# Row sums of the attention by padded ones on TensorE

## The reference

```python
q = _split_heads(query @ Wq.T + bq)      # 16 heads of 8 columns
scores = jnp.einsum('bhqd,bhkd->bhqk', q, k) / np.sqrt(D_K)
p_attn = jax.nn.softmax(scores, axis=-1)
attn = jnp.einsum('bhqk,bhkd->bhqd', p_attn, v)
x = attn.transpose(0, 2, 1, 3).reshape(B, S, D_MODEL)
return x @ Wo.T + bo
```

## Time and profile before

| what | value |
|---|---|
| runs | 1197.23, 1201.19, 1213.32 us; median 1201.19 us |
| profiled execution, its own time | 1206.03 us |
| its span, first to last instruction | 1204.3 us |
| mean granted TensorE clock | 0.878 |
| PE busy | 958.4 us (80%) |
| DVE busy | 793.0 us (66%) |
| ACT busy | 627.6 us (52%) |
| POOL busy | 579.4 us (48%) |

### The profile page before, as it was taken

The page is one execution under the profiler, slowest core; times in us unless marked ns, Lnnn a source line. Parts: engine busy times, 40 slices in busy tenths (PEclk is TensorE's granted clock), DMA queues, the critical chain, the costliest instruction groups (busy, mean ns, idle before and its releaser), DMA issues.

```text
span 1204.3 us, 18225 instructions
## 1 busy us (share of the span) xinstructions
PE 958.4 (80%) x5148; PEld 693.5 (58%) x5148; DVE 793.0 (66%) x2660; ACT 627.6 (52%) x1875; POOL 579.4 (48%) x637
## 2 busy tenths in 40 slices
PE   6440699993787888888879889888888888888883
PEld 6220588882564665566656556566656656665552
DVE  3526467653585786887789678778867867764342
ACT  2631466652344765655556556565655656643440
POOL 2477533333655347537446644744654444532223
PEclk9975799997897999989989988998998988996775
DMA  9799587661601002021011102101110200200000
GB/s 273 240 365 346 195 282 254 253 227 53 80 1 29 8 5 39 5 38 28 14 17 26 36 8 36 36 7 28 23 29 7 35 10 8 39 10 7 7 5 5
DMA packets 126519, 93.70 MB, mean 78 GB/s; under 512 B 77546, under 2 KB 105684, under 8 KB 121684
## 3 DMA queue, kind: packets, MB, share of 16 engines
q1 hardware_dynamic: 121268, 82.05, 24.9%
q0 software_dynamic: 4096, 8.40, 2.6%
q10 hardware_dynamic: 1056, 2.10, 0.6%
HBM read 59.46 MB, written 33.06 MB: 77 GB/s over the span
## 4 chain that ended last, share of the span: by engine, by line
PE 48%; DVE 19%; POOL 15%; issue 8%; ACT 7%; DMA 2%; SPq 0%; DVEq 0%; POOLq 0%; ACTq 0%
PE U L1140 5%; POOL xs_dram L526 5%; PE U L1144 5%; PE U L1141 5%; PE M L1349 4%; PE M L1343 4%; PE M L1376 4%; DVE xin L977 3%; ACT pr L779 3%; PE Y L1140 2%; PE M L1388 2%; PE Y L1144 2%; PE Y L1141 2%; PE U L1150 2%; PE OA L1361 2%
## 5 line engine op out<-in xcount | busy, mean ns | idle before, releaser
L587 POOL TENSOR_TENSOR h_lo<-h,h_hi 128x512 fp32r<-128x512 f32 x128 | 165.7, 1294 | 230.9 <-ACT h_hi L750 230.8
L779 ACT ACTIVATE pr<-M,nmax 128x128 f32<-128x128 f32 x512 | 180.4, 369 | 77.8 <-DVE nmax L1078 77.5
L1078 DVE CUSTOM_DVE_ANT_0 M<-M,mneg 128x128 f32<-128x128 f32 x512 | 132.4, 320 | 48.8 <-PE M L1343 47.8
L784 ACT ACTIVATE pT<-M 128x512 f32<-128x512 f32 x128 | 76.5, 598 | 137.1 <-PE M L1349 137.0
L1140 PE MATMUL U<-xn_hi,w_hi 128*128 128x512 f32 x256 | 130.9, 511 | 10.6 <-DVE h L1018 5.8
L1018 DVE SCALAR_TENSOR_TENSOR h<-h,U 128x512 f32<-128x512 f32 x128 | 87.4, 683 | 56.4 <-ACT h L744 56.3
L1349 PE MATMUL M<-ident,pr 128*128 128x128 f32 x512 | 96.3, 318 | 34.6 <-ACT hqT L801 18.0
L1141 PE MATMUL U<-xn_hi,w_lo 128*128 128x512 f32 x256 | 112.3, 439 | 0.0
L1144 PE MATMUL U<-xn_lo,w_hi 128*128 128x512 f32 x256 | 112.2, 438 | 0.0
L750 ACT ACTIVATE h_hi<-h 128x512 fp32r<-128x512 f32 x128 | 81.8, 639 | 48.4 <-DVE h L1022 46.8
L779 ACT ACTIVATION_READ_ACCUMULATOR pr<-M,nmax 128x1 f32 x512 | 106.8, 209 | 0.0
(11 more groups left out here) (308 smaller groups left out, 2308.8 us busy)
## 6 DMA issues: line engine op xcount, KB each, us to landing
wt<-w_dram SPq DMA_DIRECT2D x23, 1024.0 KB, 4.8
w_dram<-wt SPq DMA_DIRECT2D x8, 1024.0 KB, 7.7
xs_dram<-xr SPq DMA_DIRECT2D x1, 5888.0 KB, 19.7
ys_dram<-acc SPq DMA_DIRECT2D x12, 256.0 KB, 2.3
key_stack<-k_dram SPq DMA_DIRECT2D x48, 64.0 KB
wt<-k_dram SPq DMA_DIRECT2D x48, 64.0 KB
ys_dram<-part SPq DMA_DIRECT2D x11, 256.0 KB, 2.1
pr<-in_L_xattn_W SPq DMA_DIRECT2D x8, 256.0 KB, 6.2
```

The source lines that it names most:

```text
L587: nc.gpsimd.tensor_tensor(h_lo[i % 4][:, :], h32[i % 3][:, :], h_hi[i % 4][:, :].bitcast(fp32), ALU.subtract).then_inc(lo_done, 1)
L779: done = nc.scalar.activation(pr[i % 2][:, c], bank[:, c], ACT.Exp, bias=nmax[i % 4][:, r:r + 1], scale=-1.0, accum_out=rsum[b % 2][:, HB ...
L784: nc.scalar.activation(pT[i % 2][:, :], bank[:, :], ACT.Copy).then_inc(emptied, 1)
L1078: ins = nc.vector.tensor_tensor_reduce(bank[:, c], bank[:, c], mneg[i // HB % 2][:, :], 1.0, BIG, ALU.add, ALU.min, nmax[i % 4][:, r:r + 1])
```

## The change

A tile `ones_pad` of 24 + 32 columns is made once at the start by GpSimd: zeros, with ones in 8 columns. In each `pv` step four more matmuls follow the four products: their stationary operand is a block of 32 columns of `ones_pad` that has its 8 ones where head j of the group stands, their moving operand is the same piece of `pT`, and they write the second 128 columns of `OA`. After the four quads each of the 128 output rows has its row's sum beside it. `o` then takes the reciprocal of these 128 x 128 sums from PSUM into `rT` and multiplies. The accumulation in `exp`, the steps `rs` and `rT`, their tiles and their waits are gone.

```diff
@@ pools, POOL start
-        rsum, rinv, rwide = [sb(f"rsum{i}", [P, H]) for i in range(2)], sb("rinv", [P, H]), sb("rwide", [P, H, DK])
+        ones_pad = sb("ones_pad", [P, VPAD + CG])
...
+            nc.gpsimd.memset(ones_pad[:, :], 0.0).then_inc(ones_made, 1)
+            pool.wait_ge(ones_made, 1)
+            nc.gpsimd.memset(ones_pad[:, VPAD:VPAD + DK], 1.0).then_inc(ones_made, 1)
@@ ScalarE
-                    b, j = i // HB, i % HB
-                    if j == 0 and b >= 2:
-                        act.wait_ge(rinv_made, b - 1)
                     for r in range(HB):
                         c = slice(r * S, (r + 1) * S)
-                        done = nc.scalar.activation(pr[i % 2][:, c], bank[:, c], ACT.Exp, bias=nmax[i % 4][:, r:r + 1], scale=-1.0, accum_out=rsum[b % 2][:, HB * r + j:HB * r + j + 1])
+                        done = nc.scalar.activation(pr[i % 2][:, c], bank[:, c], ACT.Exp, bias=nmax[i % 4][:, r:r + 1], scale=-1.0)
...
-                elif what == "rT":
-                    if i >= 1:
-                        act.wait_ge(o_emptied, i)
-                    nc.scalar.activation(rT[:, :], bank[:, 0:P], ACT.Copy).then_inc(emptied, 1)
@@ VectorE
-                elif what == "rs":
-                    dve.wait_ge(*m_given_back(("s", HB * i + HB - 1)))
-                    nc.vector.reciprocal(rinv[:, :], rsum[i % 2][:, :]).then_inc(rinv_made, 1)
-                    dve.wait_ge(rinv_made, i + 1)
-                    if i >= 1:
-                        dve.wait_ge(m_full, m_at["rT", i - 1] + 1)
-                    nc.vector.tensor_copy(rwide[:, :, :], rinv[:, :].unsqueeze(2).broadcast_to([P, H, DK])).then_inc(rwide_made, 1)
                 elif what == "o":
                     dve.wait_ge(pv_done, HB * (i + 1))
-                    dve.wait_ge(*m_given_back(("rT", i)))
+                    nc.vector.reciprocal(rT[:, :], OA[:, S:2 * S]).then_inc(rinv_made, 1)
+                    dve.wait_ge(rinv_made, i + 1)
@@ TensorE
                     if j == 0:
+                        pe.wait_ge(ones_made, 2)
...
                     for r in range(HB):
                         block = VPAD + CG * (HB * r + j) - DK * j
-                        ins = nc.tensor.matmul(OA[CG * r:CG * (r + 1), 0:S], vst[b % 2][:, block:block + CG], pT[i % 2][:, r * S:(r + 1) * S], start=(j == 0), stop=(j == HB - 1))
+                        nc.tensor.matmul(OA[CG * r:CG * (r + 1), 0:S], vst[b % 2][:, block:block + CG], pT[i % 2][:, r * S:(r + 1) * S], start=(j == 0), stop=(j == HB - 1))
+                    ones = ones_pad[:, VPAD - DK * j:VPAD - DK * j + CG]
+                    for r in range(HB):
+                        ins = nc.tensor.matmul(OA[CG * r:CG * (r + 1), S:2 * S], ones, pT[i % 2][:, r * S:(r + 1) * S], start=False, stop=(j == HB - 1), skip_group_check=True)
                     ins.then_inc(pv_done, 1)
-                elif what == "rT":
-                    pe.wait_ge(rwide_made, i + 1)
-                    nc.tensor.transpose(bank[:, 0:P], rwide[:, :, :].rearrange("p h d -> p (h d)"), ident[:, :]).then_inc(m_full, 1)
```

More of the change, by code:

```diff
@@ L48 @@
          "q": 111.78, "s": 118.2, "pt": 124.25, "pv": 126.08, "wo": 147.6, "f_xt": 181.33,
-         "f_g": 184.32, "f_u": 184.68, "f_ht": 202.83, "f_dn": 210, "qs": 115, "rT": 143.5}
+         "f_g": 184.32, "f_u": 184.68, "f_ht": 202.83, "f_dn": 210, "qs": 115, }
 ACT_AT = {"xnT": -21.52, "logits": -8.93, "tanh": -0.24, "hi": 4.82, "cbc": 13.22, "nxT": 109.82, "q": 110.57,
-          "exp": 120.17, "pt": 124.92, "f_xt": 184.23, "f_g": 185.55, "f_ht": 203.96, "qs": 116, "rT": 144}
+          "exp": 120.17, "pt": 124.92, "f_xt": 184.23, "f_g": 185.55, "f_ht": 203.96, "qs": 116, }
 DVE_AT = {"mix": -37.37, "ln": -30.97, "lnx": -24.4, "xnT": -18.39, "logits": -12.72, "places": -8.44, "gated": 1.52,
@@ L54 @@
           "mask": 110.34, "q": 110.39, "max": 120.46, "o": 145.67, "wo": 149.7, "f_ln": 173.87, "f_x0": 177.59,
-          "f_x2": 179.55, "f_gu": 187.21, "f_h0": 192.03, "f_h2": 196.04, "f_dn": 212.4, "qs": 116.6, "rs": 142.5}
+          "f_x2": 179.55, "f_gu": 187.21, "f_h0": 192.03, "f_h2": 196.04, "f_dn": 212.4, "qs": 116.6, }
 POOL_AT = {"gather": -81.52, "ln": -28.71, "logits": 3.52, "lo": 4.92, "acc": 31.22, "resid": 103.86, "a_ln": 105.86,
@@ L58 @@
 SP_AT = {"x": -80, "m": 86.36, "k": 107.78, "v": 117.84, "store": 233.34}
-EACH = {"row": ("rT", "wo", "f_g", "f_u", "f_ht", "mask", "rs", "o", "f_gu", "v", "m"),
+EACH = {"row": ("wo", "f_g", "f_u", "f_ht", "mask", "o", "f_gu", "v", "m"),
         "pair": ("f_xt", "f_dn", "f_ln", "f_x0", "f_x1", "f_x2", "f_x3", "f_h0", "f_h1", "f_h2", "f_h3", "store"),
@@ L70 @@
 QUAD = GROUP / 16
-M_STEPS = {"s", "pt", "rT", "wo", "f_xt", "f_g", "f_u", "f_ht", "f_dn", "cbc", "xnT", "logits", "back", "nxT", "q", "qs"}
+M_STEPS = {"s", "pt", "wo", "f_xt", "f_g", "f_u", "f_ht", "f_dn", "cbc", "xnT", "logits", "back", "nxT", "q", "qs"}
 def later(what, i):
@@ L302, in flamingo_kernel @@
         mask_made, nmax_done, pv_done, rinv_made, o_emptied = sem("mask_made"), sem("nmax_done"), sem("pv_done"), sem("rinv_made"), sem("o_emptied")
-        vst_zeroed, rwide_made = sem("vst_zeroed"), sem("rwide_made")
+        vst_zeroed, ones_made = sem("vst_zeroed"), sem("ones_made")
         stats2, ve2_made, rstd2_done = sem("stats2"), sem("ve2_made"), sem("rstd2_done")
```

## The result

The changed kernel takes 1233.02 us (median of 4, 1230.35 to 1238.85), before in the same session 1200.97: a ratio of 1.0261 (95% interval 1.022 to 1.0303). The forecast was 1221 with a range of 1196 to 1248. The time lies in the range, 12 us above the forecast and within the forecast's own 1208 to 1234; the side is the one that had 0.41, slower by over 2%, and not "within", which had 0.54. The profiled execution of after took 1233.24 us, its span is 1231.5 us, 27.2 us longer than before's.

The account below looks back on a forecast made before the run. No engine alone was taken as the bound, but a chain going round between them. +1.66 us a group over 6.5 groups (+10.8) and the tail (+9.2) gave 1226.0 us profiled, 1221 against the median; range 1196 to 1248.

Parts of the forecast that it names:

- exponentials -0.8: On ACT, without accumulation, exponentials start 0.20 us apart instead of 0.36; credited 0.8 us a group on the chain.
- `rs` and `rT` -0.2: In the fourth sample the removed pair is 0.17 us on the chain: -0.2 us a group.
- the pair on DVE: Removing `rs` and `rT` gives back 0.61 us on DVE, counted in samples one to three of a group.
- reciprocal in `o`: On DVE, 128 columns take 0.97 us with the step to the next instruction; net of the pair, +1.40 us a group.
- the wait for ACT: In the second sample, 0.71 us of DVE idle time ahead of L995 covers the +0.36 us, so 0.
- ones: Added matmuls in `pv` on PE: 0.27 us a step, 0.45 at the lower clock level, +1.26 us a group.
- fourth sample: Nothing is given back on DVE; OT's turn comes at about 682.65 and `wo` starts later: +0.68 us.
- serial: Rival: the ones matmuls run one after another, 0.86 us a step instead of 0.27; 1248 us, chance 0.07.
- The rest: The tail: `pv` grows by 77%, +5.6 us, and six samples' `o` at 0.6, +3.6 us; together +9.2 us.
- PE as the bound: Rival: each added matmul and each longer wait for `OT` counts, 5.6 us a group; 1247 us, chance 0.19.
- A clock lifted in the tail: Rival: the added work lifts PE's clock in the last window from 0.70 to 0.91, -11 us; 1210 us, chance 0.06.
- The short reciprocal: Rival: `o` on DVE at 0.28 us, deciding from about 0.6 us down; not slower, 1201 us or 1195, chance 0.15.

Follow-up runs that it names:

- run 3: After without the ones matmuls and without the reciprocal in `o`, `rT` filled with ones, so only the removals: 1193.73 us, ratio 0.9898.
- run 2: After without the ones matmuls, the 128-column reciprocal kept and reading the products instead: 1227.02 us, ratio 1.0181.
- runs 9: After without the ones matmuls, the reciprocal cut to 16 columns: 1203.27 us, ratio 1.0003.
- run 8: After without the ones matmuls, the reciprocal cut to 64 columns: 1227.99 us, ratio 1.0176.
- run 1: After with the reciprocal cut from 128 columns to 16, ones matmuls kept: 1231.69 us, ratio 1.022.
- run 4: Before with only the ones matmuls added, their sums unused: 1207.45 us, ratio 1.0019.
- run 12: Before with one more reciprocal of 64 columns in `o`, which nobody reads: 1226.68 us, ratio 1.0187.
- run 10: After with the reciprocal cut to 16 columns and 22 unread fill matmuls a group ahead of two `pt` steps: 1204.53 us, ratio 1.0016.
- run 11: Before with 22 unread fill matmuls a group ahead of two `pt` steps: 1214.68 us, ratio 1.0108.
- runs 5: After with `wo` moved later in PE's list, behind the next s, pt and up steps: 1257.45 us, ratio 1.044.
- run 6: Before with `wo` moved later in PE's list, behind the next s, pt and up steps: 1230.06 us, ratio 1.0229.
- run 7: After with `wo` later on PE and `o` on DVE moved behind the second gating instruction L1018: 1263.89 us, ratio 1.0504.

## Why the prediction was right in the range and short by 12 us

Run 3, run 2 and after split the steady part into the prediction's terms: removals 614.7 to 609.5, reciprocal to 633.6, ones to 634.4. The prediction's terms for the same six groups, from its values for one:

| term | predicted, a group | six groups | measured |
|---|---|---|---|
| removals: exponentials -0.8, `rs` and `rT` -0.2, the pair on DVE -3 x 0.61 | -2.8 | -17 | -5.2 |
| reciprocal in `o`: 3 x 0.97 + 0.68 - 0.36 for the wait for ACT | +3.2 | +19 | +24.1 |
| ones | +1.26 | +8 | +0.8 |
| sum | +1.66 | +10 | +19.7 |

- **The failed step is the credit for the removals.** The prediction took the pair `rs` off DVE at its full length and the exponentials off the chain at a part of theirs. The pieces did leave the chain: the exponentials' share fell from 4.7 to 0.9 us a group, more than the 0.8 that was credited. But the groups without them (run 3) hardly became shorter: 102.5 on average where four of before's five had 102.65; of the 5.2 us, 3.2 come from before's one longer group. Other ways through the lists must be about as long; which they are was not traced. The prediction asked which work is overtaken only for the exponentials, and not for the 0.61 us of `rs` on DVE, of which it took back three a group.
- **The reciprocal** was sized rightly (0.956 us measured, 0.95 forecast from 6.25 ns a column and 153 ns), and so, nearly, was its cost in a group: +3.2, measured 3.4 in regular groups. The grounds were only half right. The idle time of 0.71 us did take in the second sample's part in three of after's first six groups, as forecast (in the one shown L991 starts as soon as ACT's `xn_hi` is made); in the other three, and in all six of run 2, the second sample's reciprocal is on the chain too. In the fourth sample the prediction's own terms put the turn of `OT` at 682.71 and not 682.65 (682.55 + 0.27 - 0.11), 0.06 us more a group. And a cost by length is not what runs 9, 8 and 2 show: 0.25, 0.55 and 0.96 us cost 0, 3.4 and 3.4 us a group. The page "VectorE: DVE Perf Modes" of the Trainium skill, section "First, the fixed hardware budget", gives the reciprocal a repeat count of 8. The estimate of 1.22 us worked out from that is not borne out here: 0.956 us was measured.
- **The ones** take what was forecast on PE, a little less (0.58 - 0.35 = 0.23 us a step, for 0.27), side by side and not serial. On a `pv` of the steady part that costs nothing that can be told (0.8 us in six groups on run 2; 4.9 on before). In the rest they cost 5.8 us, for 5.6 forecast: there the chain runs through most `pv`, 19 of the 25 behind 1056 us. Beside a short reciprocal they cost much more (runs 9 and 1), which no term of the prediction had.
- **The rest**: +9.2 forecast, +7.3 measured, as -8.3 for the removals, +9.8 for the reciprocal and +5.8 for the ones. The forecast had 5.6 for the ones and 3.6 for `o` net of `rs`, and nothing for the shorter exponentials.
- **What was luck.** In the steady part the ones were put 7 us too high and the removals credited 12 us too much. The two errors offset each other in part: with the reciprocal some 5 us too low, the sum is 10 us short, and not 17.
- **The exponentials** start 0.26 us apart, not 0.20.
- **The rivals.** PE as the bound (1247) did not come: run 4 adds the matmuls and stays within 0.6% of before. A clock lifted in the tail hardly came in after (0.72 for 0.70), but it did in run 4 (0.76 for 0.73), where the rest is 2 us shorter than before's with more work in it. The short reciprocal, "from a price of about 0.6 us down", had its threshold too high: without the ones it lies between 0.25 and 0.55 us, since 0.552 us still cost as much as 0.956. And with the ones it was not the way back to 1201, since run 1 lost it to the clock.

What is shown: a reciprocal in `o` makes the loss, of 128 and of 64 columns without the ones (runs 2 and 8 against 3) and of 64 in the kernel before (run 12), and with a short one beside the ones the granted clock decides (runs 1, 10, 11). The rule of the Trainium skill, "TensorE: Matmul & The Clock Gate", section "What's actually happening", that activity releases the throttle, agrees with run 10 (0.89 to 0.93 with fills); run 11 shows that fills alone, where the level has not grown, bring nothing. What stays open: through which wait the reciprocal costs its time, since runs 5 to 7 moved other waits with it; that the clock also took the saving of run 8 is argued from its windows, and no fills were run there or on after itself with its full reciprocal. Why groups so often take near 102.4, 105.8, 109.3 or 112.6 us (all five of runs 10 and 8, four of five in run 6, all five of run 7) is not settled by these runs; in runs 1 and 4 some lie between.

The tail of after, where the ones are on the chain (the shares by line from 1056 us to the end, beside the earlier trace rows):

```profile
by line: PE U L1140 14.0%; PE M L1333 8.7%; PE M L1367 8.3%; PE M L1339 7.6%; PE OA L1352 5.2%; PE M L1379 4.7%; ACT pT L784 4.5%; issue 4.2%; DVE rT L1078 3.7%; PE OA L1355 3.3%; PE M L1359 2.1%; PE M L1372 1.7%; DVE h_amax L947 1.5%; PE M
```

`pv` kept its share (5.2%, before 4.9), the ones came beside it with 3.3% of 175.5 us, 5.8 us, and the reciprocal with 3.7%, 6.5 us.

## What to carry to other kernels

In a program where engines hand work round in fixed lists, price what is added to a link without slack at its full length or more, and credit what is removed only as far as no second path of like length stands beside it: a kernel with the removal alone shows that (run 3), the last chain doesn't. Before a saving on the path to TensorE is booked, look at the granted clock of the same stretch: a shorter wait can come back as matmuls at half the clock (run 1). Where work moves from one engine to another (here sums from ACT to TensorE), ask in which layout the result arrives: without the sums, 128 columns to invert instead of 16 cost 1.8% (runs 2 and 9). A short reciprocal alone was no cure, since beside it the sums cost about as much, by way of the clock (runs 1 and 10).

## What the runs showed of the hardware

- A reciprocal on DVE costs by the column from PSUM as from SBUF: 256 ns for 16 columns, 552 for 64 and 956 for 128, against 253 for 16 in SBUF.
- An exponential of 128 columns starts every 0.26 us without accumulation and every 0.36 with it. With it, each is followed by an instruction that reads the accumulator, 512 in before, which after does not have:

```profile
L779 ACT ACTIVATION_READ_ACCUMULATOR pr<-M,nmax 128x1 f32 x512 | 106.8, 209 | 0.0
```

- More matmuls made a program faster: 148 fills, 21.0 us of PE by the rows, stand between 1231.69 us (run 1) and 1204.53 (run 10), with the granted clock up from 0.89 to 0.93. In before the same fills cost 1.1% (run 11).

```profile
L1261 PE MATMUL OA<-w_hi,ident_r 128*128 128x256 f32 x148 | 21.0, 290 | 0.0
```
